# Products nobody reads, put on TensorE in six places of a three-layer attention kernel

## What is computed

```python
x = x + cross(layernorm(x), ctx, Wq, Wk, Wv, Wo, gq, gk)   # 16 heads of 128, rmsnorm on q and k
x = x + attn(layernorm(x), W_qkv, W_out, b_out)            # 16 heads of 16; q, k, v rounded to fp8
x = x + ffn(layernorm(x), W_gate, W_qkv)                   # top-1 gate picks one head's k and v; causal
# attn: scale = max(abs(q)) / 448 over the WHOLE tensor q; the same for k and for v
```

## Time and profile before

| | us |
|---|---|
| median of 3 runs | 1449.62 |
| lowest and highest | 1449.3 and 1451.05 |
| the profiled execution's own time | 1451.55 |
| its span, from the first instruction to the last | 1449.8 |
| mean granted clock of TensorE in the span | 0.976 |

### The profile page before, as it was taken

The page is one execution under the profiler, slowest core; times in us unless marked ns, Lnnn a source line. Parts: engine busy times, 40 slices in busy tenths (PEclk is TensorE's granted clock), DMA queues, the critical chain, the costliest instruction groups (busy, mean ns, idle before and its releaser), DMA issues. The chain is left out here.

```text
span 1449.8 us, 29297 instructions
## 1 busy us (share of the span) xinstructions
PE 1372.8 (95%) x5980; PEld 938.9 (65%) x5980; DVE 1257.5 (87%) x5010; ACT 1195.8 (82%) x4845; POOL 1062.6 (73%) x1583
## 2 busy tenths in 40 slices
PE   5997999999999999999999999999999998957886
PEld 4774666666666666666666666666666666845554
DVE  6998889898989898989989898999999898766994
ACT  5897898989898989888898989898988987535673
POOL 5886789898989898898989898988889884000000
PEclk9998999999999999999999999999999999987997
DMA  3000000000000000000000000000000012000000
GB/s 139 1 21 26 1 17 8 24 2 24 1 24 1 24 1 24 8 17 20 6 24 1 24 1 24 2 24 2 24 13 16 23 30 64 2 1 1 9 12 11
DMA packets 10195, 25.35 MB, mean 17 GB/s; under 512 B 848, under 2 KB 6640, under 8 KB 9888
## 3 DMA queue, kind: packets, MB, share of 16 engines
q1 hardware_dynamic: 9728, 23.49, 4.4%
q10 hardware_dynamic: 288, 0.00, 0.0%
HBM read 22.44 MB, written 1.05 MB: 16 GB/s over the span
## 5 line engine op out<-in xcount | busy, mean ns | idle before, releaser
L1117 ACT ACTIVATE c_unused<-c_prod 124x128 f32<-124x128 f32 x1664 | 493.2, 298 | 85.4 <-DVE c_prod L1337 83.0
L1645 POOL TENSOR_TENSOR c_acc<-c_acc,c_prob 123x1024 f32<-123x1024 f32 (+1 forms) x192 | 462.4, 2408 | 40.9 <-ACT c_prob L1124 38.9
L1348 DVE CUSTOM_DVE_ANT_0 c_multiplied<-psK,c_c 124x128 f32<-124x128 f32 x1664 | 381.9, 286 | 62.7 <-PE psK L914 62.6
L913 PE MATMUL psK<-wkh,c_cTh 128*124 128x512 f32 x832 | 414.1, 498 | 3.8 <-DVE c_ss L1348 1.9
L933 PE MATMUL psO<-c_prob,raw 123*128 123x512 f32 (+1 forms) x832 | 391.7, 593 | 0.0
L914 PE MATMUL psK<-wkl,c_cTh 128*124 128x512 f32 x832 | 329.9, 397 | 0.0
L1337 DVE TENSOR_TENSOR c_prod<-psK,c_c 124x512 f32<-124x512 f32 x416 | 286.3, 688 | 40.6 <-PE psK L914 34.1
L1117 ACT ACTIVATION_READ_ACCUMULATOR c_unused<-c_prod 124x1 f32 x1664 | 311.5, 187 | 0.0
L1359 DVE TENSOR_TENSOR c_prob<-psS,c_ss 124x512 f32<-124x512 f32 x416 | 266.1, 681 | 0.7 <-POOL c_ss L1628 0.7
L1124 ACT ACTIVATE c_prob<-c_prob,shift 124x1024 f32<-124x1024 f32 x208 | 236.7, 1138 | 0.2 <-DVE c_prob L1359 0.2
L933 PEld LDWEIGHTS psO<-c_prob,raw 123*128 123x128 f32 (+1 forms) x832 | 142.1, 191 | 118.3 <-issue 99.4
(11 more groups left out here) (328 smaller groups left out, 2225.6 us busy)
## 6 DMA issues: line engine op xcount, KB each, us to landing
raw<-in_ctx SPq DMA_DIRECT2D x16, 799.5 KB
raw<-in_L_xattn_Wq SPq DMA_DIRECT2D x6, 256.0 KB, 7.4
xs<-in_x SPq DMA_DIRECT2D x4, 256.0 KB, 4.9
big<-in_L_xattn_Wk SPq DMA_DIRECT2D x1, 1024.0 KB, 7.5
c_prod<-in_L_xattn_Wo SPq DMA_DIRECT2D x1, 1024.0 KB, 5.4
out<-s_y SPq DMA_DIRECT2D x8, 128.0 KB, 1.7
big<-in_L_ffn_W_qkv SPq DMA_DIRECT2D x1, 768.0 KB, 10.2
raw<-in_L_xattn_Wv SPq DMA_DIRECT2D x1, 768.0 KB, 4.1
```

The costliest lines, as they stand in the source:

```text
L913: nc.tensor.matmul(psK[0:ROWS, c % 2, :], cTh[:, slot, :], T.wkh[:, cols], start=True, stop=False)
L1117: last = nc.scalar.activation(unused[:, j, :], prod[:, k % 2, c // 2, j * CD:(j + 1) * CD], ACT.Copy, accum_out=ss[:, k % 2, 0, h:h + 1])
L1348: last = nc.vector.tensor_tensor_reduce(multiplied[:, j, :], psK[0:ROWS, 1, cols], c2[:, k % NT, :], 1.0, 0.0, ALU.mult, ALU.add, ss[:, k ...
L1645: nc.gpsimd.tensor_tensor(acc[0:rows, batch % 2, :], acc[0:rows, batch % 2, :], prob[0:rows, probs(s), :], ALU.add).then_inc(S.acc, 1)
```

## The change

A helper issues n products of the identity with the tile of ones into a part of a PSUM bank that nothing reads. It is called in six places on PE's queue: at the end of queries (15), at the end of `end` in cross_attention (8), after the second product of the chain of maxima (20), at the head of `step(1, 0, None, None)` (12), and before the transposes of p2's probabilities in `step(None, 7, 6, 5)` (5) and in `step(None, None, 7, 6)` (12). The products signal nothing and wait for nothing. Nothing is removed or moved, and no other queue changes.

```diff
+def keep_busy(nc, T, bank, n):
+
+    for j in range(n):
+        nc.tensor.matmul(bank, T.ident[:, :], T.ones[:, :], start=(j == 0), stop=(j == n - 1))
@@ queries, tensor
             steps(step)
+            keep_busy(nc, T, psT[:, 0:P], 15)
@@ cross_attention, tensor, end
                 qkv_of(NPAIR - 1)
+                keep_busy(nc, T, psO[:, 0, 0:P], 8)
@@ self_attentions, tensor
             nc.tensor.matmul(psM[:, P:P + 3], T.ones[0:3, :], most[:, :], start=True, stop=True).then_inc(W.swept, 1)
+            keep_busy(nc, T, psO[:, 0, 0:P], 20)
...
             def step(p0, p1, p2, p3):
+                if p1 == 0:
+                    keep_busy(nc, T, psO[:, 0, 0:P], 12)
                 if p2 is not None:
                     gates_and_heads(p2)
...
                 if p0 is not None:
                     duplicate_values(p0)
+                if p0 is None and p2 is not None:
+                    keep_busy(nc, T, psO[:, 0, 0:P], 5 if p1 is not None else 12)
                 if p2 is not None:
                     transpose_pe(nc, pe, T, GS, p2, ffn_scores, prob2)
```

## The result

The changed kernel takes **1442.42 us** in the median of five runs (1440.27 to 1442.85), the kernel before 1450.5 in the five beside it. The ratio is 0.9944, 95% interval 0.9933 to 0.9955: 8.1 us faster where 5.3 had been forecast (1444.3, range 1440.0 to 1449.8). The kernel before was somewhat high in these five; beside the later runs its median is 1449.6 to 1449.9. The profiled execution's own time is 1440.27, its span 1438.5, against 1451.55 and 1449.8 before.

What follows compares the result with a forecast made beforehand. Bound: low-clock TensorE groups on the engine-to-engine chain at block ends and the self-attention's first and last steps. 0.3 + 2.9 + 2.6 + 0.5 = 6.3 us off 1451.55 gives 1445.25, adjusted for run differences to 1444.3; range 1440.0 to 1449.8.

Steps and rivals of the forecast that it cites:

- signs of being wrong: Product rows at 0.46, transposes L1802 or L1688 right behind a product, later tile loop, or unchanged clock line and time.
- The price of a product: On TensorE, one plain float32 product takes 0.24 us at the upper clock level and 0.46 us at the lower.
- Part 1: 15 products after the queries: covered but for 0.1 us; gain 0.3 us, 5.6 us the bound from above.
- Parts 2 to 4: 8, 20 and 12 products, cross-attention's end to second step: faster groups gain 2.9 us, bounds -5.0 and +6.
- Part 5: 5 products in step(None, 7, 6, 5): without the fall at 1425.8, L1838 takes 2.85 for 5.47; gain 2.6 us.
- Part 6: 12 products in step(None, None, 7, 6): between +2.5 at a high level and -1.8 at a low one, 0.5 us taken.
- The 1.0 us taken off: Whole program: about half the profiled execution's 1.93 us above the median, as runs may miss a fall; gain becomes 5.3.
- The one from the rule on transposes: First pipeline steps: transposes do not count as busy, so the level falls behind each block; sum 1.6 us.
- The first rival: First steps and end: the level falls again behind each block of products; gain 1.6 us, 1448.0; chance 0.22.
- The one in which the level holds nearly everywhere: Tile loop start, first steps and end all gain: 11.1 to 13.1 us, 1438 against the median; chance 0.12.
- The slower one: Products behind the maxima and in the second step run low, delaying transposes: 5.0 us slower, 1454.6; chance 0.08.
- part 2: 8 products at the end of the cross-attention: 1.9 us, covered, no gain by itself; an overrun costs 0.3 at most.

Runs made afterwards that it cites:

- no_b: The changed kernel without the 8 products at the end of the cross-attention: 1443.74 us, ratio 0.9959 to the kernel before.
- as_transposes: The changed kernel with each product replaced by two transposes of the tile of ones, in all six places: 1444.08 us, ratio 0.9958 to the kernel before.
- the filled one: The changed kernel plus 22 products in gaps of the first two steps and 26 in later gaps: 1438.65 us, and 1438.14 us when run again.
- c_double: The changed kernel with 40 in place of 20 products behind the chain of maxima: 1446.92 us, ratio 0.9978 to the kernel before.
- ef_only: The kernel before plus only the 5 and 12 products in the two last steps: 1446.24 us, ratio 0.9972.
- no_a: The changed kernel without the 15 products behind the queries: 1441.85 us, ratio 0.9952 to the kernel before.
- changed_again: The changed kernel, unaltered, run and profiled a second time: 1443.28 us, ratio 0.9952 to the kernel before.

## Why the prediction was right, point by point

- **What bounds the kernel.** Right: the time came from the groups of PE on the chain at the ends, and no other queue changed. The list of low stretches was not complete: the one at 1214 is missing in it, and with it a place for products. Two of the signs of being wrong did appear, L1688 right behind a product in the first profile and L1802 right behind one in `no_b`; the pushes were 0.57 and 1.6 us, less than the change gains in those steps.
- **The price of a product.** Right, 0.24 us at the upper level (40 rows in 4.73 us); blocks that met the lower one came to 0.29 to 0.38 us a product on average (3.46 to 4.57 us for 12, 7.52 for 20).
- **Part 1, 15 products, 0.3 us.** Neither shown nor refuted: alone they gave 0.65 us, with an interval that holds nothing. The cover held: from the last product of L470 to the first tile transpose is 4.40 us without them and 4.39 with them. As foreseen, the level fell a few us later instead (at 127.8 to 131.8 in seven profiles with them, at 120.4 to 125.2 in four without). The second low stretch, which I had priced within the 5.6 us bound, comes or not in either case.
- **Parts 2 to 4, 2.9 us.** Right in size: 3.05 alone. The chance of a push behind the 12 was real (0.57 us in the first profile, 7.08 against 6.51). The path was right in part: the sum took the projection L1827 as fast (0.94 us) and the level as lost behind it. In four of seven profiles it was lost ahead of the projection, which took 2.02 us, and the heads were slow too; in the others the projection was fast and the heads were low for a part or the whole of their length. That the median meets the sum is therefore in part luck.
- **Part 5, 2.6 us.** Right in mechanism, and by the profiles in size: 1.9 to 3.0 us.
- **Part 6, 0.5 us.** By the profiles this term was too small. The tail is 13.93 or 13.06 us without the products, 11.21 with them at the upper level, and 11.8 to 12.1 where they or the scores in front of them ran low: 1.0 to 2.7 us. The step "up to 5.5 us, 1.8 too long" took them as low throughout; the longest took 4.57, and the tail's L1688 came only 0.65 us late (5.44 against 4.79 us behind the first of L1678), as the level was back by their end. Parts 5 and 6 were never run apart; together they gave 3.6 us in the medians against 3.1 in the sum.
- **The 1.0 us taken off** because runs of before might miss a fall: not borne out. No profile without parts 5 and 6 was without that fall, and the parts alone add up to 7.3 us, 1.0 over the sum of 6.3. The first 8.1 us hold some luck besides: the second time it was 6.65.
- **The rivals.** The one from the rule on transposes is refuted by `as_transposes`. The first rival is not borne out: behind the block of 12 the level held for up to 10 us of short groups, though it did fall again before the heads were done, and the last heads took 7.1 us in every profile with the five products. The one in which the level holds nearly everywhere was worked out as 1438 us; the changed kernel does not reach it, but the filled one does, at 1438.1 and with the gaps closed. The slower one has the right price (`c_double`, `no_b`) and lacks its condition: part 2 carries the level over the chain of maxima.
- **The two profiles' 11.3 us** are 8.1 or 6.7 of the change, and for the rest draws: 1.6 us of tile stage, 0.4 of cross, up to 1.1 of last heads and 1.4 of pair 0, each of which varies by about as much between profiles in which that place has the same code.

What stays open: whether part 1 is worth anything at all, why three runs of `ef_only` gained nothing, and whether a fall that the filled kernel still has can be closed with profit, as DVE is late there.

## What to carry to other kernels

Where a chain goes from engine to engine and TensorE works in short groups, look at its granted clock before looking at the groups: a level of 0.50 over the chain nearly doubles them (eight transposes took 1.97 us for 1.04), and filling the waits with products nobody reads can win it back if each block is shorter than its wait at the upper level. Look for every wait behind which the level falls and fill the short ones too: this gave 5.1 us more here. The 15 products ahead of the tile loop, where PE has to wait for other engines, showed no gain that can be told from chance. Compare medians of several runs, since one profile of such a kernel holds 1 to 4 us of luck in where the level falls.

## What the runs showed of the hardware

- Transposes of float32 (of a tile of ones) in the gaps held the upper level over 17 us in which PE did otherwise only short groups, as products did at the same places (granted clock 1.00 from 1291 to 1308.7 in `as_transposes`), against the expectation from the rule.
- The level was back by the end of every block of 12 or 20 products that met the lower one (once 0.3 us behind it): 40 rows that began low took 7.52 us (`no_b`), 24 rows that began low 3.47 and 3.46 (`ef_only`, `no_a`), and 24 rows within which it fell 4.57 in three executions (the first profile, `changed_again`, `c_double`). Wholly low they would be 9.2 and 5.5 us, an estimate from 0.46 a product. That the products bring it back is likely, as the same place in the kernel before was low for 30.6 us, but a low stretch as short also ended without them (142.3 to 145.6 in the kernel before).
- The two kernels with two profiles had their low stretches at other places in the second, but behind the same few gaps; stages in which the level is the same repeat within some 0.05 us.
